# A decoder block on one core: the last key blocks of two heads mixed together, and a changed order of work at three places

## The reference, cut to what matters

```python
def reference(x, ctx, Wq, Wk, Wv, Wo, scales, A_w, B_w, Wq_w, keys):  # x 2x512x1024, ctx 2x1024x1024
    x = x + attn(layernorm(x))
    x = x + matmul(fake_quant(layernorm(x)), fake_quant(ctx))
    return x + experts(layernorm(x))

def attn(h):                      # 32 query heads, 8 key/value heads, head size 128, causal
    q, k, v = h @ Wq, h @ Wk, h @ Wv          # 1024x4096, 1024x1024, 1024x1024
    q, k = rope(q), rope(k)
    p = softmax(causal(q @ k.T / sqrt(128)))
    return (p @ v) @ Wo                       # 4096x1024

def fake_quant(x):
    return (clip(round(x / s + z), 0, 255) - z) * s

def experts(x):                   # 64 experts of rank 8, 16 of them taken for each row
    gate = softmax(top_16(x @ Wq_w.T @ keys.T))
    return ((x @ A_w.T) * gate) @ B_w.T * 2
```

## Time and profile before

| | |
|---|---|
| time, median of 3 runs | 1297.61 us |
| lowest and highest | 1295.29 and 1298.22 us |
| the profiled execution's own time | 1296.9 us |
| its span | 1295.1 us |
| PE busy, share of the span | 98% (6929 matmuls) |
| PEld, weight loads beside the matmuls | 84% |
| DVE busy | 65% |
| ACT busy | 59% |
| POOL busy | 47% |
| mean granted clock of TensorE | 0.997 |
| HBM traffic over the span | 182 GB/s |

### The profile page before, as it was taken

The page is one execution under the profiler, slowest core; times in us unless marked ns, Lnnn a source line. Parts: engine busy times, 40 slices in busy tenths (PEclk is TensorE's granted clock), DMA queues, the critical chain, the costliest instruction groups (busy, mean ns, idle before and its releaser), DMA issues. The chain is left out here.

```text
span 1295.1 us, 19782 instructions
## 1 busy us (share of the span) xinstructions
PE 1262.9 (98%) x6929; PEld 1085.7 (84%) x6929; DVE 835.9 (65%) x1866; ACT 767.2 (59%) x1577; POOL 609.0 (47%) x450
## 2 busy tenths in 40 slices
PE   9999999999999999999999998999999999998998
PEld 8898998888888888888888887878888887766887
DVE  7774735556556656656556565655786788788763
ACT  4412247767777877777777877863333355565530
POOL 4777666779758777677766754420000000021100
PEclk9999999999999999999999999999999999999999
DMA  8033245558659568486485678758874486201111
GB/s 276 25 131 123 79 134 188 155 138 210 218 151 244 164 169 244 133 204 169 118 237 143 158 221 259 212 177 259 283 200 128 152 273 217 79 7 29 50 42 49
DMA packets 122403, 208.74 MB, mean 161 GB/s; under 512 B 15408, under 2 KB 56368, under 8 KB 118720
## 3 DMA queue, kind: packets, MB, share of 16 engines
q1 hardware_dynamic: 118272, 178.10, 42.5%
q0 software_dynamic: 4032, 29.36, 12.2%
HBM read 147.40 MB, written 88.08 MB: 182 GB/s over the span
## 5 line engine op out<-in xcount | busy, mean ns | idle before, releaser
L1253 DVE TENSOR_TENSOR pT_lo<-banks,pT_hi 128x512 fp32r<-128x512 f32 (+1 forms) x192 | 103.6, 595 | 170.7 <-ACT pT_hi L984 170.7
L1665 PE MATMUL banks<-ob_hi,oa_hi 128*128 128x512 f32 x384 | 149.5, 389 | 0.9 <-DVE ob_lo L1293 0.9
L1665 PE MATMUL banks<-ob_hi,oa_lo 128*128 128x512 f32 x384 | 149.4, 389 | 0.0
L1665 PE MATMUL banks<-ob_lo,oa_hi 128*128 128x512 f32 x384 | 149.4, 389 | 0.0
L1623 PE MATMUL banks<-xc,nring_hi_a 128*128 128x512 f32 x448 | 139.9, 393 | 2.1 <-DVE q_made L1203 2.1
L1623 PE MATMUL banks<-xc,nring_hi_b 128*128 128x512 f32 x448 | 139.5, 392 | 0.0
L968 ACT CAST oa_hi<-oraw 128x1024 fp32r<-128x1024 f32 x48 | 50.4, 1050 | 142.9 <-PE banks L1665 129.1
L984 ACT CAST pT_hi<-banks 128x512 fp32r<-128x512 f32 (+1 forms) x192 | 86.6, 527 | 66.0 <-PE banks L1593 66.0
L1879 POOL TENSOR_TENSOR resid<-resid,colterm 128x1024 f32<-128x1024 f32 x8 | 19.0, 2379 | 216.6 <-ACT colterm L1937 137.5
L737 POOL TENSOR_TENSOR q_lo<-q_raw,q_hi 128x512 fp32r<-128x512 f32 x64 | 87.0, 1360 | 38.5 <-ACT q_hi L921 38.2
L1578 PE MATMUL banks<-kT,q_hi 128*128 128x512 f32 (+2 forms) x384 | 104.2, 352 | 0.0
(11 more groups left out here) (256 smaller groups left out, 3413.8 us busy)
## 6 DMA issues: line engine op xcount, KB each, us to landing
q_raw<-qk_dram SPq DMA_DIRECT2D x64, 256.0 KB, 4.2
o_S<-o_st SPq DMA_DIRECT2D x64, 256.0 KB, 4.0
w<-in_L_attn_Wo SPq DMA_DIRECT2D x32, 512.0 KB, 5.9
oraw<-o_S SPq DMA_DIRECT2D x32, 512.0 KB, 3.7
nraw<-in_L_attn_Wq SPq DMA_DIRECT2D x28, 512.0 KB, 5.3
o_S<-o_S POOLq DMA_DIRECT2D x12, 1024.0 KB, 10.0
o_S<-o_N POOLq DMA_DIRECT2D x12, 1024.0 KB, 10.2
resid<-in_x SPq DMA_DIRECT2D x16, 512.0 KB, 7.1
```

Source lines behind the costliest of these rows:

```text
L1253: nc.vector.tensor_tensor(pT[1][:, sl], turned_chunk(turned, mixed, c), as32(pT[0][:, sl]), ALU.subtract).then_inc(pT_lo, 1)
L1665: ins = nc.tensor.matmul(step_bank(m, t), oa[a][:, s % 2, k, t * P:(t + 1) * P], ob[c][:, s % 2, k, :], start=(q == 0 and k == 0 and i == ...
```

## The change

1. **Pairs.** What the last key block (`TPB - 1`, seen by the last 128 query rows alone) takes of an even unit's probabilities is kept in `pT` beside that of the odd unit that follows. `mix` of an even unit leaves the block out. `mix` of an odd unit ends with three matmuls of 256 columns that read both blocks (`last_blocks`, two blocks of 128 columns that lie 512 apart) into bank `turned[:, 1]`. DVE adds the results (`add_pair`): the odd unit's to `mixed`, the even one's to its rows in `o_st[0]`. ACT's copy of the odd unit, PE's second chunk of the next even unit and SP's store of the even unit wait for that. SP stores the even unit's rows at the end of its iteration instead of in the middle.
2. **Buffers.** `pT` grows from 1280 to 1408 columns, `small` shrinks from 256 to 16, `first_mask` moves into `prob`, and `identb` and `one` share their memory with `pair_kept`, so POOL makes them after the last pair and not at the start.
3. **Start.** 70 transposes instead of 72, PE waits for `ident` alone, and tile 1's statistics move from DVE to ACT, as sums over `Identity` and `Square`.
4. **Entry into the steps.** `load_first(2)` moves to the head of iteration 57, `first_high(1)` on ACT from iteration 56 to 57, behind `probs_high(56)` and the casts of q, and POOL's order of `first_low` follows. After unit 63, `load_step(0)` and `load_step(1)` stand before `keep_out(62)`.
5. **Experts.** ACT and DVE get another order around tiles 1 to 3; PE's list there is unchanged.

```diff
-WARM = 72
+WARM = 70
-KEYS_AT = {0: 0, 1: 512, 3: 896, 2: 1024}
-CHUNKS = ((0, (0,)), (512, (1, 3)), (1024, (2,)))
+CHUNK_KEYS = ((0,), (1, 3), (2,))
 CHUNK_WIDTH = (512, 512, 256)
+PT = 1408
@@ shared
-        identb = sb("identb", [P, P], BF16)
+        late = sb("late", [P, 2, P], BF16)
+        identb, one = late[:, 0, :], late[:, 1, :]
+        pair_kept = late[:].rearrange("p n c -> p (n c)").bitcast(F32)
+    def keys_at(u, j):
+        return {0: 0, 1: 640, 2: 1152, 3: 1024 if u % 2 else 512}[j]
+    def chunk_at(u, c):
+        return (0, 640 if u % 2 else 512, 1152)[c]
+    def last_blocks(part):
+        return pT[part][:].rearrange("p (k c) -> p k c", c=P)[:, 4:9:4, :]
@@ SP
         def keep_out(u):
             sp.wait_ge(o_copied, u + 1)
+            if u % 2 == 0:
+                sp.wait_ge(pair_added, u // 2 + 1)
...
+            if u == LAST_JOB_UNIT + 1:
+                load_first(2)
...
-            if u >= 2:
+            if u >= 2 and u % 2:
                 keep_out(u - 2)
...
             for f in steps_of(u + 1):
-                if f >= 2:
+                if f >= 3:
                     load_first(f)
...
-        keep_out(UNITS - 2)
+            if u >= 2 and u % 2 == 0:
+                keep_out(u - 2)
         load_step(0)
         load_step(1)
+        keep_out(UNITS - 2)
         keep_out(UNITS - 1)
@@ POOL
-        pool.wait_ge(ident_made, 1)
-        nc.gpsimd.tensor_copy(identb[:], ident[:]).then_inc(ident_made, 1)
-        nc.gpsimd.memset(one[:], 1.0).then_inc(one_made, 1)
...
-            for f in steps_of(u + 1):
-                first_low(f)
-                if f == 0:
-                    turn_added(JOBS - 1)
+            if u == LAST_JOB_UNIT:
+                first_low(0)
+                turn_added(JOBS - 1)
+            elif u == LAST_JOB_UNIT + 1:
+                for f in range(1, 4):
+                    first_low(f)
+            else:
+                for f in steps_of(u + 1):
+                    first_low(f)
...
+        pool.wait_ge(pair_added, UNITS // 2)
+        nc.gpsimd.tensor_copy(identb, ident[:]).then_inc(ident_made, 1)
+        nc.gpsimd.memset(one, 1.0).then_inc(one_made, 1)
@@ ACT
+        def ln_stats(t):
+            act.wait_ge(x_in[t], 16)
+            link(nc.scalar.activation(raw[:, 0, :], resid[:, t, :], ACT.Identity, accum_out=moments[:, t, 0:1]))
+            link(nc.scalar.activation(moments[:, t, 0:1], moments[:, t, 0:1], ACT.Identity, scale=1.0 / D))
+            link(nc.scalar.activation(lnw[:, 2, t:t + 1], moments[:, t, 0:1], ACT.Identity, scale=-1.0))
+            link(nc.scalar.activation(raw[:, 0, :], resid[:, t, :], ACT.Square, bias=lnw[:, 2, t:t + 1],
+                                      accum_out=moments[:, t, 1:2]))
+            nc.scalar.activation(moments[:, t, 1:2], moments[:, t, 1:2], ACT.Identity, scale=1.0 / D
+                                 ).then_inc(act_stats, 1)
...
         def keep_out(u):
             act.wait_ge(mix_done, u + 1)
+            if u % 2:
+                act.wait_ge(pair_added, u // 2 + 1)
...
+        ln_stats(1)
         root(0)
...
+            if u == LAST_JOB_UNIT + 1:
+                first_high(1)
...
-            if (u + 1, 1) in STEP_AT:
+            if (u + 1, 1) in STEP_AT and u > LAST_JOB_UNIT:
                 first_high(STEP_AT[u + 1, 1])
@@ DVE
+        def add_pair(u):
+            dve.wait_ge(o_copied, u)
+            dve.wait_ge(mix_done, u + 1)
+            link(nc.vector.tensor_copy(pair_kept, turned[:, 1, P:2 * P]))
+            nc.vector.tensor_tensor(mixed[:, H - P:H], mixed[:, H - P:H], pair_kept, ALU.add)
+            nc.vector.tensor_tensor(o_st[0][:, H - P:H], o_st[0][:, H - P:H], turned[:, 1, 0:P],
+                                    ALU.subtract if batch_of(u) else ALU.add).then_inc(pair_added, 1)
...
-        for t in range(TPB):
+        for t in (0, 2, 3):
             ln_stats(t)
+        dve.wait_ge(act_stats, 1)
...
             normalise(u)
+            if u > 0 and u % 2 == 0:
+                add_pair(u - 1)
...
             step_low(s)
+            if s == 0:
+                add_pair(UNITS - 1)
@@ PE
-        pe.wait_ge(ident_made, 2)
+        pe.wait_ge(ident_made, 1)
...
             for c in range(3):
+                if c == 1 and u > 0 and u % 2 == 0:
+                    pe.wait_ge(pair_added, u // 2)
...
-            for j in range(TPB):
+            for j in range(TPB - 1):
                 w = H - j * P
...
+            if u % 2:
+                for p, (a, c) in enumerate(PASSES):
+                    ins = nc.tensor.matmul(turned[:, 1, 0:2 * P], vv[a][:, h % 2, TPB - 1, :], last_blocks(c),
+                                           start=(p == 0), stop=(p == 2))
@@ experts, ACT: tiles 1 and 2 written out
         highs("x", (2, 3))
+        high("z", 0)
         root(2)
         normalise(2)
-        for i in range(1, TT):
...
+        highs("b", range(6, 8))
+        read_product(3)
+        scale_tile(4)
+        exponentials(1)
+        highs("x", (4, 5))
+        read_product(4)
+        root(3)
+        high("z", 1)
+        normalise(3)
+        scale_tile(5)
+        for i in range(2, TT):
@@ experts, DVE: tile 1 written out
         product_stats(2)
+        low("z", 0)
         scale_of(2)
+        row_term(3)
         late_scale(0)
-        for i in range(1, TT):
...
+        lows("b", range(6, 8))
+        add_product(3)
+        quantise(4)
+        row_term(4)
+        gate(1)
+        add_out(0, 0)
+        lows("x", (4, 5))
+        add_out(0, 1)
+        product_stats(3)
+        add_product(4)
+        scale_of(3)
+        low("z", 1)
+        for i in range(2, TT):
...
-            if i == 1:
+            if i == 2:
                 late_stats(TPB + 2)
                 late_stats(TPB + 3)
```

More of the change, by code:

```diff
@@ L132, in build @@
         scl = sb("scl", [P, 2, TT], F32)
-        one = sb("one", [P, P], BF16)
         banks = whole.enter_context(nc.psum_tensor("banks", [P, 8, 512], F32))
@@ L154, in build @@
             prob = sb2("prob", [P, 1280], F32)
-            pT = [sb2(f"pT_{n}", [P, 1280], F32R) for n in ("hi", "lo")]
-            small = sb2("small", [P, 256], F32)
+            pT = [sb2(f"pT_{n}", [P, PT], F32R) for n in ("hi", "lo")]
             n_sin = sb2("n_sin", [P, H], F32)
@@ L175, in build @@
             mask = sb2("mask", [P, H], F32)
+            small = sb2("small", [P, 16], F32)
             heads = (kv_raw, q_raw, [q_first, q_second], q_made, prob, pT, small, mask, o_st, kT, k_both, vv)
@@ L257, in attention @@
 def attention(nc, held, es, x_t, Wq, Wk, Wv, Wo, cos_in, sin_in, quant_in, ctx_rows, qk_dram, v_dram, o_dram,
-              A_w, B_w, proj, heads, narrow, outp, resid, ident, identb, stats, moments, rstd, lnw, mean_rstd, scal,
+              A_w, B_w, pair_kept, proj, heads, narrow, outp, resid, ident, identb, stats, moments, rstd, lnw, mean_rstd, scal,
               calc, scl, one, raw, a_rows, b_rows, q2, banks, KT, TT, TPB, H):
@@ L269, in attention @@
     shift, total, inv = (small[:, n:n + 4] for n in (0, 4, 8))
-    first_mask = small[:, P:2 * P]
+    first_mask = prob[:, PROB_AT[0]:PROB_AT[0] + P]
     score = banks[:, 0:3, :]
@@ L281, in attention @@
     ident_made, mask_made = sem("ident_made"), sem("mask_made")
-    pool_link, dve_link = sem("pool_link"), sem("dve_link")
+    pool_link, dve_link, act_link = sem("pool_link"), sem("dve_link"), sem("act_link")
+    act_stats = sem("act_stats")
     var_ready, root_ready, scaled_mean = sem("var_ready"), sem("root_ready"), sem("scaled_mean")
@@ L878, in _ @@
     def _(act):
+        link = Links(act, act_link)
+        def ln_stats(t):
[7 more added lines that the diff above has]
+                                 ).then_inc(act_stats, 1)
         def root(n):
@@ L983, in probs_high @@
                     act.wait_ge(mix_done, u)
-                nc.scalar.copy(pT[0][:, CHUNKS[c][0]:CHUNKS[c][0] + CHUNK_WIDTH[c]],
+                nc.scalar.copy(pT[0][:, chunk_at(u, c):chunk_at(u, c) + CHUNK_WIDTH[c]],
                                turned_chunk(turned, mixed, c)).then_inc(pT_hi, 1)
@@ L1250, in probs_low @@
             for c in range(3):
[L1251 removed]
+                sl = slice(chunk_at(u, c), chunk_at(u, c) + CHUNK_WIDTH[c])
                 dve.wait_ge(pT_hi, 3 * u + c + 1)
@@ L1589, in turn_probs @@
                 dst = turned_chunk(turned, mixed, c)
-                for j in CHUNKS[c][1]:
+                for j in CHUNK_KEYS[c]:
                     for i in range(j, TPB):
-                        col = KEYS_AT[j] - CHUNKS[c][0] + (i - j) * P
+                        col = keys_at(u, j) - chunk_at(u, c) + (i - j) * P
                         ins = nc.tensor.transpose(dst[:, col:col + P],
@@ L1604, in mix @@
                     ins = nc.tensor.matmul(mixed[:, j * P:H], vv[a][:, h % 2, j, :],
-                                           pT[c][:, KEYS_AT[j]:KEYS_AT[j] + w],
```

(46 more changed lines are left out.)

6 lines of the change are left out of this document (2 added, 4 removed).

## The result

| kernel | median us | lowest and highest | runs | ratio to the kernel before, 95% interval |
|---|---|---|---|---|
| before | 1297.61 | 1295.17 to 1298.22 | 5 | |
| changed | 1306.05 | 1305.58 to 1312.48 | 5 | 1.0078 (1.0060 to 1.0096) |

The change made the kernel slower by 0.8%, where 0.7% faster had been forecast. The span of the profiled execution is 1303.9 us, 8.8 more than before.

The account below looks back on a forecast made before the run. PE was taken to bound the kernel, busy 582 of 589 us in attention. Terms -5.4 + 0.9 + 0 - 0.1 - 4.3 = -8.9 us on a 1295.1 span gave 1286.2, a median of 1288.7; range 1286 to 1291, with rivals 1282.5 to 1293.5.

Parts of the forecast that it names:

- the store order: SP's even-unit store after the sum, at the end of its list: costed at 0, with a 3.9 us median landing.
- Rival D: Even store does not land before ACT wants its buffer: 1317 if eight units land like the worst; chance 0.05.
- The paired mix: Attention units: three 256-column matmuls replace 128-column ones, 0.20 us less a pair, 6.3 for 32; term -5.4 us.
- Rival B: In the paired mix, strided 256-column matmuls cost more: 4 us back, 1292.7; chance 0.10.
- What the pairing adds: DVE's sums mostly hidden behind jobs; 0.4 us shows in unit 50, 0.5 at step 1: +0.9, at most 3.
- The entry: Unit 57: PE's 3.2 us wait goes, but load 3 may come late; taken as 0, between -3.5 and +2.6.
- The start: Kernel start: fewer warm-up transposes and tile 1's statistics on ACT, but DVE sets the first product; term -0.1 us.
- rival E: At the start, Sqrt's table costs one more load length (1.28 us), 1.0 late: 1289.7; chance 0.03.
- The expert stage: Reordered ACT and DVE: -3.6 up to multiply(4), -1.6 from full clock, +0.9 new wait; -4.3 us, bounds -5.3 and -2.
- The new wait before multiply(6): Expert stage: late_stats(6) and (7) move one round back, so add_out(2,0) ends late and PE waits 0.9 us.

Follow-up runs that it names:

- e2: The changed kernel without the pairs, their sums and waits; the even unit's store stays at the end of SP's iteration: 1305.97 us, ratio 1.0070.
- e3: The changed kernel without the pairs and with the even unit's store back in the middle of SP's iteration: 1294.95 us, ratio 0.9981.
- e4: The changed kernel with the expert-stage order of ACT and DVE of the kernel before: 1309.25 us, ratio 1.0091.
- e7: The changed kernel with POOL adding tile 6's column term only after DVE has quantised tile 6: 1308.21 us, ratio 1.0081.
- e8: The changed kernel with late_stats(6) and (7) on DVE moved back ahead of product_stats(3): 1308.24 us, ratio 1.0082.
- e5: The changed kernel with POOL's third accumulating transfer of each group of heads issued one unit later: 1295.69 us, ratio 0.9983.
- e10: e5 with pairs only up to unit 47 and the even store in the middle of SP's iteration from unit 48: 1289.23 us, ratio 0.9943.
- e1: The changed kernel with the even unit's store back in the middle of SP's iteration, pairs kept: 1302.46 us, ratio 1.0046.

## Why the prediction was wrong

**The step that failed is the one on the store order, "I cost it at 0".** It cost 11.0 us (e2 against e3) on the forecast of -8.9. Rival D named the mechanism and got its place in the list wrong. It had the store issued 0.9 us after the odd unit's mix, with 9.7 us of room. In fact the store stands last in SP's iteration, behind what SP still waits for: for the stall in unit 21 it was issued 4.5 us after the sum, with 5.2 us to ACT's next use, where a landing of 11.6 us is far too late. The prediction read the landing times as a distribution, a median of 3.9 and a worst of 15.3, and gave the worst 5 in 100. They are mostly no chances: in the traces of all five kernels with the late store and POOL's old order (changed, e2, e4, e7, e8) the stores of units 18, 42 and 50 are issued 0.8 to 1.6 us behind POOL's third 1 MB transfer and land after 9.2 to 13.2 us, and in e5 they don't. Before the change too the stores beside these transfers landed late (unit 19's after 12.7 us, 1.0 ahead of its next use). What had to be read was which transfer each even store would now be issued behind.

**The paired mix** (6.3 us before deductions) was sized too low for a pair. Where nothing disturbs it the changed kernel wins 0.31 us and not 0.20: the three matmuls take 0.35 for the two units against 2 x 0.283, and the first job behind 128-column matmuls ran 0.07 slower before, which the prediction left out by ending its measure at the next matmul's start. But not every pair wins it: up to mix(49) e5 gains 5.7 us on e3, where 25 pairs make 7.8 at 0.31 and 5.0 at 0.20, as units 3, 19, 20, 27, 33 and 47 gain nothing or lose up to 0.4 us. So the sum came out nearer to the forecast than its price. Rival B (the stride) is refuted by the 0.117 us spacing. The Trainium skill ("TensorE: Matmul & The Clock Gate", Back-to-back issue gap) has a sustained spacing of about 81 ns at N=128, against 94 here; it would have made the term smaller, and the rows go further the other way.

**What the pairing adds** was put at +0.9, at most 3. It was 5.5 in units 50 to 56 and 1.0 in the steps (e5 against e3), confirmed by e10. Unit 50 was named, at 0.4; it took 0.9, since the transposes wait twice. Units 52 and 55 weren't, though the list of units without a second job was at hand, and neither was the clock behind a wait, 2.1 of the 5.5 us, which falls in some executions and not in others.

**The entry** was taken at 0 in -3.5 to +2.6. The wait of PE's mix fell by 3.4 us, and 0.65 of clock with it; 1.3 + 0.8 came back in unit 58, where ACT waited 2.1 us for `oraw`: -1.9, as e3 shows too.

**The start** was right in size, -0.1 against 0.0: DVE's low parts start 0.4 us earlier, at 14.30, as tile 2 lands at 7.3, and the products give it back by 38 us. (The -0.4 at mix(0) comes off a wait for ACT behind them.) Sqrt's load was hidden, with the row of ACT at 9.10 (1.28 us) and Sqrt at 10.66 behind DVE: rival E is refuted. So is, here, the drain of 1.38 us that the Trainium skill ("ScalarE: Activation LUTs", What ACT_TABLE_LOAD costs) adds to each switch, by which Sqrt could not have started before 11.8.

**The expert stage** was put at -4.3 and gave -0.5 up to its last matmul. The first part is right: -5.3 up to the fills behind multiply(4), 5.2 forecast. The new wait before multiply(6) was foreseen at 0.9; it was 3.3, and 1.5 to 1.7 of clock behind it. 2.2 of the wait is POOL's addition, which the prediction left out, as no row of DVE before is stretched by more than 0.3 us: `scale_tile` releases POOL and DVE at the same instant, and in tile 6 POOL came 0.02 us ahead. The Trainium skill ("SBUF — State Buffer", Who interferes with whom) has an exclusive lock between the two, which whoever issues first holds for its whole instruction, against DVE's `tensor_scalar` in the two-port modes and its `tensor_tensor` with two inputs in SBUF. This case's rows agree, though none says in which mode the TENSOR_SCALAR ran: 2.92 us behind POOL's 2.39, 2.23 for a TENSOR_TENSOR of one column, and POOL's 2.83 instead of 2.36 where DVE had started first (tile 4).

Against the terms of the sum, the store order is 11.0 us off, what the pairing adds 5.6, the expert stage 3.8, the entry -1.9, the end behind the last matmul -1.2 and the pairs about -1: 16 of the 17.4 us between forecast and measurement; for the rest no cause is shown. The forecast erred by adding up gains on PE and treating the queues as unchanged. With the collision away (e5) the changed kernel stands at 1295.7, with the uncovered pairs away as well at 1289.2.

## What to carry to other kernels

When an edit gives a buffer's store a later release, compute its issue from its place in the issuing engine's list, not from the release, and look up which big transfers will be on the queues then: here a store issued 3.3 us later, with no transfer more, turned a landing in time into a stall. A sum that two engines wait for is free only where independent work lies between its producer and its users; go through the irregular rounds by name. Where two engines are released by one event and one of them is on the path, order them by hand.

## What was not expected of the hardware

- A one-column TENSOR_TENSOR on DVE took 2.23 us instead of 0.16 beside POOL's addition of 2.40 us, and moving the addition a little later moved the block to the next such operation.
- The clock after a wait is not the same each time. In unit 26 PE waits 1.77 us before a job both in the kernel before and in e3; the job then takes 3.01 us in the one and 4.57 in the other, as the same window of both shows (the kernel before, then e3):

```profile
478.00:484.00 6.00, 5.88 (x34) 5.21 (x35) 1.90 (x6) 5.69 (x12) 5.26 (x6) 1.00 0.97 296
478.00:484.00 6.00, 6.00 (x27) 4.92 (x26) 0.74 (x2) 4.21 (x11) 4.25 (x4) 0.72 1.00 309
```

- It is so in the expert stage too: a wait of 1.9 us before multiply(4) was followed by 5.30 us of multiply in the profile before and by 3.61 in that of e4, one of 3.1 before multiply(6) by 5.30 (e1) and by 3.61 (e2).
- Three matmuls of 256 columns over two blocks 512 columns apart ran 0.117 us apart, no slower than contiguous ones (0.12).
